# One recommendation model on one core: gathers released by landed rows, a first pair written out by hand, and a block of the deep network moved

## The reference

```
emb = tables[feat_idx, sparse]                        # (512, 26, 32)
linear_out = lin_sparse_w[feat_idx, sparse].sum(-1) + dense @ lin_dense_w
x0 = xk = emb
for w, bb in ((conv1_w, conv1_b), (conv2_w, conv2_b)):   # 128 outputs each
    hp = einsum('bhd,bmd->bhmd', xk, x0).reshape(-1, h * 26, 32)
    xn = sigmoid(einsum('oi,bid->bod', w, hp) + bb)
    xk = xn[:, :64]; res.append(xn[:, 64:])
cin_out = concatenate(res).sum(-1) @ cin_w + cin_b
h1 = tanh(concat(emb.reshape(-1, 832), dense) @ W1 + b1)    # 1024
h2 = tanh(h1 @ W2 + b2); h3 = tanh(h2 @ W3 + b3)            # 512, 256
out = linear_out + cin_out + h3 @ deep_w + deep_b + bias
```

## Time and profile before

| | us |
|---|---|
| median of three runs | 447.75 |
| the profiled execution | 447.28 |
| its span, from the first to the last instruction | 445.5 |
| TensorE busy | 423.0 |
| VectorE busy | 318.5 |
| ScalarE busy | 161.1 |
| GpSimd busy | 164.2 |
| mean granted clock of TensorE | 0.981 |

### The profile page before, as it was taken

One profiled execution on the slowest core, in us unless ns is written; L12 is line 12 of the kernel. 1 busy time (PEld: TensorE's weight loads), 2 busy tenths in 40 slices (PEclk: granted clock), 3 DMA queues, 4 the chain that ended last, 5 costly groups with the idle time before them and its releaser, 6 DMA issues.

```text
span 445.5 us, 5390 instructions
## 1 busy us (share of the span) xinstructions
PE 423.0 (95%) x1961; PEld 176.5 (40%) x1961; DVE 318.5 (71%) x356; ACT 161.1 (36%) x264; POOL 164.2 (37%) x146
## 2 busy tenths in 40 slices
PE   3687989999999999999999999999999989999997
PEld 3662322333233332323333333323333225887784
DVE  3104568898989898988989898989889794522121
ACT  3027224444352634444453526344443321111011
POOL 6734516243343516172434436060000096840000
PEclk9978789999999999999999999999999999999999
DMA  5445477787878686877877686949657631310000
GB/s 189 91 113 119 100 181 168 186 198 171 184 187 194 171 205 162 192 181 175 196 176 190 179 195 157 227 125 211 183 148 162 146 94 47 97 48 1 0 0 0
DMA packets 38304, 64.03 MB, mean 144 GB/s; under 512 B 19601, under 2 KB 22033, under 8 KB 38278
## 3 DMA queue, kind: packets, MB, share of 16 engines
q1 hardware_dynamic: 34694, 61.93, 54.7%
q0 software_dynamic: 3584, 1.76, 4.2%
HBM read 61.96 MB, written 1.71 MB: 143 GB/s over the span
## 4 chain that ended last, share of the span: by engine, by line
PE 74%; DVE 11%; issue 11%; ACT 2%; SPq 1%; DVEq 0%; another core or an unknown queue 0%; DMA 0%; ACTq 0%
PE conv L434 32%; PE conv L412 18%; PE conv L491 7%; PE ring L491 7%; DVE copied L696 7%; PE ring L424 5%; PE ring L396 3%; DVE prod L696 3%; ACT sq L573 1%; ACT xk L544 0%; ACT sq L533 0%; DVEq L694 0%; PE conv L510 0%; PE conv L506 0%
## 5 line engine op out<-in xcount | busy, mean ns | idle before, releaser
L348 POOL DMA_INDIRECT emb<-in_table,rows x112 | 128.3, 1146 | 168.8 <-DMA laid<-emb 137.1
L696 DVE TENSOR_TENSOR prod<-ring,xk 128x1024 f32<-128x1024 f32 x112 | 133.8, 1218 | 38.0 <-PE ring L424 29.1
L696 DVE TENSOR_TENSOR copied<-copied,xk 128x1024 f32<-128x1024 f32 x96 | 114.2, 1230 | 0.4
L434 PE MATMUL conv<-prod,w_sb 128*64 128x512 f32 x448 | 114.4, 614 | 0.1
L434 PE MATMUL conv<-copied,w_sb 128*64 128x512 f32 x384 | 96.3, 603 | 2.9 <-DVE copied L696 2.0
L412 PE MATMUL conv<-sq,w_sb 117*64 117x512 f32 x384 | 90.4, 606 | 0.3 <-issue 0.3
L544 ACT ACTIVATE xk<-conv,const_sb 64x512 f32<-64x512 f32 x64 | 43.7, 682 | 126.3 <-PE conv L412 113.1
L533 ACT ACTIVATE sq<-ring 117x512 f32<-117x512 f32 x90 | 48.5, 595 | 31.5 <-PE ring L396 19.5
L434 PEld LDWEIGHTS conv<-copied,w_sb 128*64 128x64 f32 x384 | 24.7, 137 | 67.3 <-issue 38.3
L412 PEld LDWEIGHTS conv<-sq,w_sb 117*64 117x64 f32 x384 | 27.8, 139 | 55.9 <-issue 55.7
L434 PEld LDWEIGHTS conv<-prod,w_sb 128*64 128x64 f32 x448 | 26.7, 137 | 51.3 <-issue 43.4
(11 more groups left out here) (76 smaller groups left out, 292.2 us busy)
## 6 DMA issues: line engine op xcount, KB each, us to landing
copied<-laid SPq DMA_DIRECT2D x192, 256.0 KB
wpiece<-in_mlp SPq DMA_DIRECT2D x22, 256.0 KB
emb<-in_table,rows POOLq DMA_INDIRECT x112
raw<-laid SPq DMA_DIRECT2D x32, 52.0 KB
laid<-emb SPq DMA_DIRECT2D x16, 96.0 KB, 2.9
sel_f<-in_sel SPq DMA_DIRECT2D x1, 832.0 KB, 5.6
const_sb<-in_const SPq DMA_DIRECT2D x1, 626.0 KB, 4.1
w_sb<-in_w SPq DMA_DIRECT2D x1, 416.0 KB, 6.2
```

The lines of the kernel that those rows point to most:

```text
L348: pool.indirect_dma_start(out=emb[0:n, i, j, :], out_offset=None, in_=table, in_offset=bass.IndirectOffsetOnAxis(ap=rows[0:n, i, j:j + 1], ...
L434: mm = nc.tensor.matmul(conv[i % 2][c * HALF:(c + 1) * HALF, :], w2_sb[:, t, :], prod_of(r)[:, c, :], start=(t == 0), stop=(t == T2 - 1))
L696: nc.vector.tensor_tensor(prod_of(r)[:, :, :].rearrange("p c n -> p (c n)"), left[:, :, :].rearrange("p c n -> p (c n)"), xk[i % 2][:, :, ...
```

## The change

`gather(i)` waits for the rows of the pair in front to have landed, where it waited, from pair 2 on, for their layout. The tiles in `COPIED` are 2, 3, 6, 7, 10, 11 (tile 1 is spread now, 11 copied), with six buffers instead of five. Tile 1 of the next pair is spread behind tile 11, beside tile 0. Pair 0 leaves the loop and is written out: each of the three sums of pair 1 has a tile of pair 0 behind it, and layer1(1, 0) and (1, 1) stand behind tile 3 and spread 12. On ScalarE the rounding of x(1) stands behind both sigmoids of pair 0, on VectorE x_low(1) behind tile 1. 13 dummies of 512 columns in float32 over the whole array take the place of the 113. The first block of the deep network stands behind tile 7 of the last pair, and its matmuls wait for `xt_lo` one part at a time. `lin_row` lies over `xt`, and `clamped` over `wrap`.

```diff
-COPIED = (1, 2, 3, 6, 7, 10)
+COPIED = (2, 3, 6, 7, 10, 11)
-RC = 5
+RC = 6
+DEEP_AT = 1
-SPREADS_IN = (((0, 4), (0, 5)), ((0, 8), (0, 9)), ((0, 11), (0, 12)), ((1, 0),))
-SUMS_IN = ({0: ((1, 0), (1, 1), (1, 2)), 2: ((2, 0),), 3: ((2, 1),)},
-           {0: ((1, 2),), 2: ((2, 0),), 3: ((2, 1),)})
-L1_AHEAD = ({0: 0}, {})
-L1_IN = ({0: 1}, {0: 0, 1: 1})
+SPREADS_IN = (((0, 4), (0, 5)), ((0, 8), (0, 9)), ((0, 12), (1, 0)), ((1, 1),))
+SUMS_IN = {0: ((1, 2),), 2: ((2, 0),), 3: ((2, 1),)}
+L1_IN = {0: 0, 1: 1}
-WARM = 113
+WARM = 13
...
-                if i >= 2:
-                    pool.wait_ge(laid_in[(i - 1) % RX], LAID * ((i - 1) // RX + 1))
+                if i:
+                    pool.wait_ge(rows_in[(i - 1) % GSEM], ROWS * ((i - 1) // GSEM + 1))
...
+            def deep(layer, mt):
+
+                hi, lo, kt, xh, xl = deep_layers[layer]
+                start = sum(MT[:layer])
+                n = start + mt
+                if n >= 2:
+                    pe.wait_ge(tanh_done, n - 1)
+                for k in range(kt):
+                    if n == 0:
+                        pe.wait_ge(xt_lo_done, k + 1)
...
+            pe.wait_ge(sel_in, 16)
+            for k in range(WARM):
+                nc.tensor.matmul(conv[1][:, :], sel2_f[:, 0, :], sel2_f[:, 0:4, :].rearrange("p t o -> p (t o)"),
+                                 start=True, stop=True)
             pe.wait_ge(sel_done, 1)
-            for k in range(WARM):
-                nc.tensor.matmul(conv[1][0:UK, 0:2 * UK], sel1_sb[:, 0, :], sel1_sb[:, 0:2, :].rearrange("p u k -> p (u k)"),
-                                 start=True, stop=True)
...
-            spread_tile(0)
+            spread_tile(SPREAD[0])
+            spread_tile(SPREAD[1])
             layer1(0, 1)
             pe.wait_ge(w2_in, 16)
-            for i in range(NPAIR):
+            for u in range(UT):
+                sums_of(1, u)
+                main(u)
+            spread_tile(SPREAD[2])
+            main(3)
+            spread_tile(SPREAD[3])
+            layer1(1, 0)
+            for r in SPREAD[4:-1]:
+                spread_tile(r)
+            for t in range(4, 8):
+                main(t)
+            spread_tile(SPREAD[-1])
+            layer1(1, 1)
+            for t in range(8, T2 - 1):
+                main(t)
+            for k in range(2):
+                sums_of(2, k)
+                spread_tile(T2 + SPREAD[k])
+            main(T2 - 1)
+            for i in range(1, NPAIR):
...
+                    if i == NPAIR - 1 and g == DEEP_AT:
+                        pe.wait_ge(piece_lo, KW)
+                        pe.wait_ge(l2_read, NPAIR - 1)
+                        deep(0, 0)
...
             sigmoid(0, 0)
+            sigmoid(0, 1)
             x_high(1)
-            sigmoid(0, 1)
...
-            x_low(1)
...
+                    if i == 0 and t == 1:
+                        x_low(1)
```

More of the change, by code:

```diff
@@ L125, in build @@
         emb = sb("emb", [P, NPAIR, GJ, ROW])
+        at_xt = space(0)
         xt = sb("xt", [P, K1, B])
+        lin_row = sb("lin_row", [1, B], F32, at_xt)
         idx_sb = sb("idx_sb", [P, 2, NPAIR, GJ], I32)
@@ L201, in sums_in @@
         def sums_in(i, g):
-            return [(i + ahead, u) for ahead, u in SUMS_IN[min(i, 1)].get(g, ()) if i + ahead < NPAIR]
+            return [(i + ahead, u) for ahead, u in SUMS_IN.get(g, ()) if i + ahead < NPAIR]
         def spreads_in(i, g):
@@ L242, in build @@
             enter(("sums", 0, u))
-        enter(("spread", 0))
-        for i in range(NPAIR):
+        enter(("spread", SPREAD[0]))
+        enter(("spread", SPREAD[1]))
+        for u in range(UT):
+            enter(("sums", 1, u))
+        for r in SPREAD[2:]:
+            enter(("spread", r))
+        for k in range(2):
+            enter(("sums", 2, k))
+            enter(("spread", T2 + SPREAD[k]))
+        for i in range(1, NPAIR):
             for g in range(len(GROUPS)):
@@ L436, in main @@
                 mm.then_inc(main_done, 1)
+            deep_layers = ((m1_hi, m1_lo, K1, xt_hi, xt_lo), (m2_hi, m2_lo, K2, h1_hi, h1_lo),
+                           (m3_hi, m3_lo, K3, h2_hi, h2_lo))
+            def deep(layer, mt):
[7 more added lines that the diff above has]
+                        pe.wait_ge(xt_lo_done, k + 1)
+                    if layer and mt == 0:
+                        pe.wait_ge(h_lo_done, start - kt + k + 1)
+                    r = K1_LAST if layer == 0 and k == K1 - 1 else P
+                    for j, (w, h) in enumerate(((hi, xh), (lo, xh), (hi, xl))):
+                        mm = nc.tensor.matmul(MLP_BANKS[n % 2], w[0:r, k, mt * P:(mt + 1) * P],
+                                              h[0:r, k, :], start=(k == 0 and j == 0),
+                                              stop=(k == kt - 1 and j == 2))
+                mm.then_inc(mlp_done, 1)
             pe.wait_ge(const_in, 16)
@@ L473, in _ @@
                              start=False, stop=True).then_inc(lin_done, 1)
[L475 to L478, removed]
[L479 to L495 removed]
+            for layer in range(3):
+                pe.wait_ge(piece_lo, (KW, KW + K2, PIECES)[layer])
+                for mt in range(1 if layer == 0 else 0, MT[layer]):
+                    deep(layer, mt)
                 if layer == 0:
```

27 lines of the change are left out of this document (5 added, 22 removed).

## The result

| | before | after |
|---|---|---|
| median, us | 447.75 (444.98 to 449.23, 5 runs) | 431.92 (430.31 to 432.29, 5 runs) |
| the profiled execution | 447.28 | 432.29 |
| its span | 445.5 | 430.4 |

The account below looks back on a forecast made before the run. It took TensorE to bound the middle pairs (20.3 of 20.4 us) and VectorE the last. Start -10.5 and deep block -1.8 gave -12.3: 447.28 to 435.0, plus 0.47 for the median, 435.4 us; range 430.5 to 441.5.

Parts of the forecast that it names:

- the start's term: Up to pair 1: it starts at 58.7 instead of 69.24, -10.5 us, bounds -15.1 to -4.6.
- Dummies, and the start: Start: long dummies end at 20.9 us, squares of pair 0 start at 22.0 instead of 31.08, 9.1 us earlier.
- Gathers: Gathers run ahead from pair 3 on; DMA share goes from 0.77 to 0.83, cost 0.
- Steady pairs: Middle pairs: same work, cost 0, bounds -0 to +0.3 us a pair, that is +4.2.
- Deep block in the last pair: End: the moved block saves 4.9 us behind the pair and adds 3.1 in it, -1.8 us, bounds -3.2 to 0.
- the +3.1 by which the pair grows: Last pair: with the deep block inside, its tiles end at 375.3 instead of 372.2 us.
- (c): Rival, steady pairs: spread 5's slot waits every pair for product (next,1); slower, 449.5 us at 1 us a pair; chance 0.04.
- (d): Rival, start: dummies run at half clock and end at 33, only the tail gains; 447 us; chance 0.04.
- (a): Rival, pair 0: late instructions or low clock through tile 3 cost about 5 us; 440.5 us; chance 0.20.
- (b): Rival, start and tail: no low clock in pair 0, xt_lo ready sooner; 431.3 us; chance 0.10.

Follow-up runs that it names:

- c1: The kernel before, unedited, run and profiled again: 438.6 us, ratio 0.9999 to before in its set.
- c2: The kernel after, unedited, run again on one chip beside before: 430.84 us, ratio 0.9814 to before.
- e4: The kernel after with the 113 small dummies of before instead of the 13 long ones: 431.96 us, ratio 0.9828 to before.
- e8: The kernel after with gathers that don't wait for the rows in front: 431.54 us, ratio 0.9845 to before.
- e3: The kernel after with the gathers' old wait for layouts, from pair 2 on: 434.04 us, ratio 0.9866 to before.
- e1: The kernel after with the tile order of before (tile 1 copied, 11 spread, only tile 0 spread ahead): 436.8 us, ratio 0.994 to before.
- e2: The kernel after with the first deep block back behind the last tile: 433.54 us, ratio 0.9861 to before.
- e6: The kernel after with 20 float32r matmuls filling TensorE's idle time in pair 0: 436.32 us, ratio 0.9895 to before.
- e10: The kernel after with 250 dummies of 64 columns instead of the 13 long ones: 435.27 us in one run.

## Why the prediction was right, and where it was wrong

The total came out 3.5 us below the forecast and inside the range. A part of that is luck: the start's term was 2.4 us too large and the middle's 4.25 too small, and the start's term existed only because the recorded runs of before had a gap that the kernel doesn't have elsewhere.

*Dummies, and the start.* Right in what happens: no gap, squares at 22.7 (22.0 forecast), x_low(1) done at 34.9 (34.3), a low clock behind it. Wrong by 2.4 us in the sum, and all of it arises behind the idle time: TensorE takes up the sums of pair 1 at 34.30, where I had 34.4. Tiles 0 and 1 at the low clock take 1.97 each and end at 40.1, not 38.8. Up to layer1(1, 0), at 43.59 and not 41.8, it is 1.8 us late. Ahead of tile 11 it waits 0.61 us for VectorE's product, which I didn't have. The dummies cost nothing of this, but I had misread them: 1.06 us each is a mean of 1.71 at first and 0.86 then, and 0.133 for the small ones is a mean too. So the clock of 1.00 in the earlier trace rows didn't mean that TensorE ran at its full pace from 8.5 us on. But the term holds only against the recorded before. Against the same kernel without its gap (c1, 59.81) the start gains nothing (59.85 in c2; the 61.10 of the recorded after is 1.3 later than c2): the -10.5 was the removal of 9.4 us that were there in one set of runs. The reason I gave for the gap, instructions late behind the copies, could not be confirmed: e4 puts the same 113 dummies back and has none, and the packet that I looked for comes only after the gap has ended. Without the gap I had 23.5 for the end of the small dummies; c1 has 22.6 and e4 23.0. The rule that I weighed is in the Trainium skill, "Runtime: NRT & Kernel Launch", Instruction fetch mechanics: crossing a block of instructions is mostly hidden. c1 and e4 agree with it; whether the gap of the recorded profile goes against it isn't known, since nothing shows that TensorE was waiting for instructions there. Open: what decides whether the gap appears (the chip, how the program is loaded, or something else), and whether after is safe from it by its long dummies or was lucky; the one profile of after from the set in which before had it shows none, and no later one does.

*Gathers.* Right: no cost (e8, and the steady pairs), and perhaps some gain in late x's (e3, 2 us in pair 1 of its profile).

*Steady pairs.* This step failed: "Cost 0, bounds -0 (TensorE 20.32 of 20.38)". I read the busy time of the matmul records as TensorE's load, and took 20.3 as a floor. The records' ends are modelled and run over a wait, so a stretch can look full while weight loads wait for VectorE. e1 undoes this edit alone and has 20.38 again; the edit is worth 0.37 us a pair, and the 13 periods from pair 1 to pair 14 are 4.8 us shorter in c2 than in c1. The prediction itself had half of it, "with one product in hand VectorE gains slack", and didn't ask who had been waiting for that slack. It also says that no row of the waits of that stretch has TensorE waiting for another engine. That was misread: weight loads are TensorE's, and the same view of before, 74 to 340 us, from which the earlier trace rows shows one line, has this one too:

```profile
PEld conv L434 <- DVE copied L696: 19.0, 32, 0.9
```

*Deep block in the last pair.* Right in mechanism: TensorE waits for the last `xt_lo` and goes on at once. Mis-sized: -1.8 forecast, -2.7 measured by the profiles of the result. The term that was off is the +3.1 by which the pair grows: it grew by 2.1. I had taken the place and length of `xt_lo` over from before, and its seven took 12.8 us and not 14.2, because the new order of tiles has one copied product less beside its first part (e1 has 14.2 again). So the last part made TensorE wait 0.51 us. e1 and e2 together show that this gain belongs to the block and the tile order jointly: 0.9 us for the block with the old tiles, 0.4 for the tiles with the old block, 2.6 for both (c1's 91.2 against 88.6). That the two engines disturb each other holds the other way round too: two pairs of VectorE's copied products take 3.55 and 3.62 beside `xt_lo`, one of each pair 1.3 to 1.4 and the other 2.3, and a pair of them in the middle of the kernel 2.35.

*Rivals.* (c) is refuted: no pair waits for product (next,1), and the periods fell. (d) would have been the case had before been measured without its gap: the start wasn't cut, and yet the middle and the end gave 7.8. (a) is true in part (the low clock until 40.7, where I had 39) at 2.4 us rather than 5. (b) has nearly the right time, 431.3, by a wrong way: it wanted 13.2 at the start.

## What to carry to other kernels

Before calling TensorE the bound of a stage because its busy time fills it, read the waits of its weight loads, and compare the time of one tile with that of a tile whose operand is long there; 0.37 us in a pair were hidden in rows that read 20.32 of 20.38. Take the engine's name from such a wait and not the price: two profiles of one program gave totals of 16.8 and 33.6 us for the same loss. Two parts of a change can be worth more together than apart (0.9 and 0.4 us, together 2.6), so take out each of them alone before giving a part its share. A gap that no engine or DMA explains should be seen in a second profile of the same kernel before a change is priced on it: here it was over half of the measured gain (9.4 us between two profiles of before, 445.5 and 436.1, where the change gives 7.8 without the gap) and belonged to that set of runs. Time won early (e6's 2.9 us) must be followed to the next loads in the queue, which need not be earlier for it.

## What was unexpected of the hardware

- The same program took 445 to 449 us in one set of runs and 437 to 442 in three others, on three chips; between the two profiles, one of each kind, the difference is a hole of 7 us in TensorE's work at 18 to 25 us and what hangs on it.
- TensorE's first matmuls run at half pace under a clock column that reads 1.00: dummy records every 0.86 us until 12.93, then every 0.43 us.
- TensorE's granted clock falls behind quite short idle times at the start: 0.52 over 34.3 to 40.7 behind 4.68 us of idleness in after, 0.57 over 22 to 30 behind 4.67 us in e10. With 20 matmuls in between it stays full (e6, 1.00 over 34.3 to 43.6), which brought pair 1 forward by 2.9 us.
- VectorE's copied products, 1.18 us each, take 1.3 and 2.3 us by turns beside GpSimd's `xt_lo` in after (3.55 and 3.62 for two). The first three of the last pair of before take 1.17 to 1.21 each there; it is `xt_lo`'s first part that takes 3.73 us in their place, where a part that meets no copied product takes 1.29.
